# A stage-by-stage recurrence with a feed-forward net in its gaps: p's rows in three pieces, low parts moved ahead, output parts placed among the h32 stages

## What is computed

```python
# q, p: [8, 512]; drive: x[:, t, :], t = 0..255; dt = 0.01
def derivative(q, p, drive):
    dq = q - q ** 3 / 3.0 - p + drive + jnp.tanh(q) @ coupling.T + bias
    dp = 0.08 * (q + 0.7 - 0.8 * p)
    return dq, dp
# 256 steps of the classical four-stage Runge-Kutta method, q and p clipped to +-20 after each
# q_trace: [8, 256, 512], the q after every step
w_gu, w_down = dequant_fp4(gate_up), dequant_fp4(down)      # 2816 x 512, 512 x 1408
gate, up = split(q_trace @ w_gu.T)
y = (silu(gate) * up) @ w_down.T
out = x + y / sqrt(mean(y * y, axis=-1) + 1e-6)
```

## Time and profile before

| | |
|---|---|
| median of 3 runs | 1520.15 us (1519.74 to 1520.77) |
| the profiled execution | 1519.87 us, span 1518.0 us |
| busy: PE, PE's weight loads, DVE, ACT, GpSimd | 94%, 93%, 95%, 47%, 1% |
| instructions on DVE | 10781 |
| chain that ended last | PE 89% (L518 53%, L295 22%, L307 14%), DVE 5% |
| PE products of the recurrence (L518) | 32768, mean 175 ns |
| granted TensorE clock | 0.999 over the span |

### The profile page before, as it was taken

The page is one execution under the profiler, slowest core; times in us unless marked ns, Lnnn a source line. Parts: engine busy times, 40 slices in busy tenths (PEclk is TensorE's granted clock), DMA queues, the critical chain, the costliest instruction groups (busy, mean ns, idle before and its releaser), DMA issues.

```text
span 1518.0 us, 90291 instructions
## 1 busy us (share of the span) xinstructions
PE 1424.1 (94%) x36992; PEld 1408.7 (93%) x36992; DVE 1434.8 (95%) x10781; ACT 718.9 (47%) x4836; POOL 12.2 (1%) x38
## 2 busy tenths in 40 slices
PE   0277999999999999999999999999999999999998
PEld 0166999999999999999999999999999999999998
DVE  6999999999999999999999999999999999999991
ACT  2144445445454544545454454545445455544541
POOL 0000000000000000000000000000000000000000
PEclk9999999999999999999999999999999999999999
DMA  9500000000000000000000000000000000000000
GB/s 243 138 7 4 15 7 8 22 8 21 4 8 21 8 21 8 21 4 7 21 8 22 7 22 4 8 21 8 22 8 21 7 4 22 7 21 8 22 4 22
DMA packets 13520, 32.67 MB, mean 22 GB/s; under 512 B 1712, under 2 KB 6064, under 8 KB 12976
## 3 DMA queue, kind: packets, MB, share of 16 engines
q1 hardware_dynamic: 13104, 26.89, 6.7%
HBM read 22.69 MB, written 4.19 MB: 18 GB/s over the span
## 4 chain that ended last, share of the span: by engine, by line
PE 89%; DVE 5%; ACT 0%; issue 0%; POOLq 0%; DVEq 0%; POOL 0%; ACTq 0%
PE scan_ps L518 53%; PE gu_ps L295 22%; PE y_ps L307 14%; DVE th L590 1%; DVE q_stage L626 1%; DVE with_q L584 1%; DVE q_stage L628 1%; DVE q_sq L594 0%; DVE scan_ps L602 0%; DVE p_part L584 0%; DVE q_cub L597 0%; DVE with_p L584 0%; ACT th L556 0%; DVE q_raw L628 0%; DVE q_raw L626 0%
## 5 line engine op out<-in xcount | busy, mean ns | idle before, releaser
L518 PE MATMUL scan_ps<-th,wscan 128*128 128x32 f16 (+1 forms) x32768 | 1015.9, 175 | 87.6 <-ACT th L556 87.0
L518 PEld LDWEIGHTS scan_ps<-th,wscan 128*128 128x128 f16 x32768 | 937.9, 96 | 102.6 <-ACT th L556 95.1
L556 ACT ACTIVATE th<-q_stage 128x16 f16<-128x16 f32 x1536 | 318.5, 207 | 527.6 <-DVE q_stage L626 527.6
L295 PE MATMUL gu_ps<-hist,wffn 128*128 128x128 f32 x2816 | 503.3, 284 | 0.0
L295 PEld LDWEIGHTS gu_ps<-hist,wffn 128*128 128x128 f32 x2816 | 393.9, 192 | 0.0
L590 DVE TENSOR_TENSOR th<-t,th 128x16 f16<-128x16 f32 x2048 | 352.6, 172 | 1.1 <-ACT t L558 0.6
L307 PE MATMUL y_ps<-wffn,h 128*128 128x128 f32 x1408 | 323.6, 313 | 0.0
L558 ACT ACTIVATE t<-q_stage 128x16 f32<-128x16 f32 x1536 | 305.8, 199 | 0.0
L556 ACT ACTIVATE th<-q_raw 128x16 f16<-128x16 f32 x512 | 106.2, 207 | 220.8 <-DVE q_raw L626 182.6
L307 PEld LDWEIGHTS y_ps<-wffn,h 128*128 128x128 f32 x1408 | 209.5, 189 | 0.4 <-DVE h L323 0.4
L373 ACT ACTIVATE sum_r<-dr,constant 128x64 f32<-128x64 f32 x528 | 174.1, 332 | 7.8 <-DMA dr<-drive 7.8
(11 more groups left out here) (33 smaller groups left out, 539.3 us busy)
## 6 DMA issues: line engine op xcount, KB each, us to landing
raw<-packed SPq DMA_DIRECT2D x11, 768.0 KB, 9.0
dr<-drive SPq DMA_DIRECT2D x34, 128.0 KB, 2.5
sc<-scales SPq DMA_DIRECT2D x11, 384.0 KB, 9.3
xres<-x SPq DMA_DIRECT2D x16, 256.0 KB, 3.5
out<-osb SPq DMA_DIRECT2D x16, 256.0 KB, 2.9
coup<-coupling_t SPq DMA_DIRECT2D x1, 1024.0 KB, 15.0
q_raw<-cond_t SPq DMA_DIRECT2D x1, 16.0 KB, 1.6
bias<-bias_t SPq DMA_DIRECT2D x1, 2.0 KB, 1.7
```

What stands on the lines that cost most here:

```text
L295: i = nc.tensor.matmul(gu_ps[b][:, half * P:(half + 1) * P], wffn[:, u, j * P:(j + 1) * P], hist[1 - f.parity][:, kt].rearrange("p t b -> ...
L518: i = nc.tensor.matmul(to if both else to[:, 0], wscan[:, w, part, kt, cols], moving if both else moving[:, 0], start=first, stop=last, sk ...
L556: nc.scalar.activation(th[s % 2][:, c, 0, :], q[:, c, :], ACT.Tanh, scale=1.0 / S).then_inc(now.tanh_hi, 1)
```

## The change

`add_p` is cut in three: rows 1 and 2 (64 elements) at the head of a step's first stage, row 3 (32 elements) behind the last additions of the second stage, row 0 (32 elements) where all four stood, in the last stage of the step before. The third stage's first instruction now waits for row 3. In a step's last stage the order becomes `low_part` 0, p4, `low_part` 1, `cube`. `norm_out` may only take stages that are 1 modulo 4 and have no `h32` in either block: 81, 93, 109 and 121, that is 17, 29, 45 and 57 of the next block. With them, the wait for `other_cleared` moves from step 12 to step 15 (stage 60). DVE has 22 counted instructions for each step in place of 20.

```diff
-LOCALS = STEPS * 20
+LOCALS = STEPS * 22
...
-        first = self.norm_sum + 3
-        first += -first % 4
-        self.norm_out = {first + 4 * n: n for n in range(KT)}
+        taken = {s % STAGES for s in ready}
+        free = [s for s in range(self.norm_sum + 3, 2 * STAGES) if s % 4 == 1 and s % STAGES not in taken]
+        self.norm_out = {s: n for n, s in enumerate(free[:KT])}
...
-            def add_p(step):
-                p_rows = p_state[:, :, :].unsqueeze(1).to_broadcast([P, ROWS, KT, B])
-                return add(with_p[:, :], p_rows, P_ALL, sum_r[:, step % STEPS])
+            def add_p(step, first, rows):
+                p_rows = p_state[:, :, :].unsqueeze(1).to_broadcast([P, rows, KT, B])
+                return add(with_p[:, first:first + rows], p_rows, P_ALL, sum_r[:, step % STEPS, first:first + rows])
...
-                if t == STEPS - 4 and before:
+                if t == STEPS - 1 and before:
                     dve.wait_ge(now.other_cleared, 1)
                 if t == 0 and before:
                     dve.wait_ge(before.local, LOCALS)
-                ffn_part(s)
+                add_p(t, 1, 2)
...
                 add_q(with_q2[0], 2, BY_Q2, q2, with_q1[1][:, :, :])
+                row3 = add_p(t, 3, 1)
                 finish(s)
 
                 s = 4 * t + 2
+                dve.wait_ge(now.local, row3)
                 add_q(with_q1[2], 3, BY_Q1, q1, with_p[:, 3])
-                ffn_part(s)
...
                 squared = square(3, q4)
+                low_part(s, 0)
                 p4 = add(p_part[3][:, :, :], p_part[2][:, :, :], P_SUM[3], q4)
-                low_part(s, 0)
+                low_part(s, 1)
                 dve.wait_ge(now.local, squared)
                 cubed = cube(3, q4)
-                low_part(s, 1)
...
-                add_p(t + 1)
+                add_p(t + 1, 0, 1)
                 finish(s)
```

## The result

The changed kernel takes **1573.84 us** (median of 4 runs, 1569.38 to 1576.39) against 1520.28 us (1519.74 to 1520.77), a ratio of 1.035 with a 95% interval of 1.032 to 1.038: 53.6 us slower. The profiled execution took 1576.39 us with a span of 1574.6. Its runs are 7 us apart, those of the kernel before 1 us; what is known of that is told under parts_only.

The account below looks back on a forecast made before the run. A loop of reduce, tanh on ACT, low parts on DVE and PE's products sets each stage. 1519.9 - 10.1 (gains) + 47.7 (wait) + 15.4 (clock) = 1572.9, about 1573 us; 8 in 10 range 1553 to 1588.

Parts of the forecast that it names:

- the chain: Last output part, store, xres load, GpSimd's clear, then DVE's wait: 7.5 us (7.0 to 8.2), with three stages to run.
- case (c): Rival: xres lands up to 1 us a block later beside the drive's load, clock pays twice; 1593 us, chance 0.07.
- Case (b): Rival: GpSimd's clear is early, chain under 4.1 us, DVE does not stand at stage 60; 1510 us, chance 0.05.
- the wait: DVE stands 3.4 us at stage 60 in each of blocks 2 to 15, 47.7 us in all (40 to 57).
- case (d): Rival: pieces cost what they bring, the 10.1 us gain goes, wait as forecast; 1583 us, within the forecast's 0.60.
- Clock: PE's clock gate falls to half rate in the stage 60 waits, in up to 14 places; 15.4 us.
- case (a): Rival: the wait is there but the clock stays up; 1558 us (1550 to 1567), chance 0.27.
- The last stage: Each step's last stage: 0.03 us saved, 0.02 at steps 7 and 15, 0.06 in block 0; 7.9 us together.
- The pieces: Rows 1 and 2 free before the clip; row 3 fits the second stage's gap, 0.6 us in all behind h32.
- a later clip: At step 1, expected to roughly cancel the second wait removed at step 12.
- The output parts: Moved from first to second stages: a block pays 0.24 us in place of 0.42, 2.5 us saved (1 to 5).
- Gains: Wanted part of the change: 7.9 from last stages + 2.5 from output parts - 0.3 = 10.1 us.

Follow-up runs that it names:

- parts_only: Kernel before with only the output parts in stages 17, 29, 45 and 57 and the other_cleared wait at step 15; 1576.85 us, ratio 1.038.
- parts_early: Changed kernel with the four output parts in stages 17, 29, 33 and 45 instead of 17, 29, 45 and 57; 1508.37 us, ratio 0.992.
- no_low_parts: parts_early with p4, low part 0, cube, low part 1 back in their old order; 1515.90 us, ratio 0.9974.
- keep_busy: Changed kernel plus 12 unused f32 products on PE at stage 60 of blocks 2 to 15, inside the wait; 1556.90 us.
- load_first: Changed kernel with SP issuing the load of xres ahead of the store of osb, not behind its landing; 1509.80 us, ratio 0.993.
- early_parts_only: Kernel before with only its output parts in stages 17, 29, 33 and 45 and the wait at step 15; 1517.77 us, ratio 0.9986.

## Why the prediction was right, and where it was off

**Mechanism.** Each link of the chain stood as predicted. The blocked instruction starts 7.46 us after the output part in the block shown (7.55 predicted), and only in blocks 2 to 15. Over these it is 7.08 to 8.84, where 7.0 to 8.2 was said: GpSimd's wait reaches 8.23 us in one block, over the 7.60 read from the kernel before, while the median went down. So case (c), that the chain grows because the drive's load runs beside it, shows in the median not at all. Case (b), a clear that comes early, is refuted by the wait itself, and case (d), pieces that cost what they bring, by parts_early and no_low_parts. keep_busy and parts_early put the wait at 48.5 us against 47.7, load_first shows that its length is the two transfers in a row, and parts_early that nothing of it is lost when they have time.

**Clock.** Predicted at 1.1 us for each wait, 15.4 in all; keep_busy gives 16.9, or 1.2 each, and 17.9 with the fall that it still has. Of the 1.2 some 0.2 lie in stage 60 itself, whose last products come at the lower level (5069 against 4810 ns, of which 0.07 us are DVE's longer wait). The granted clock fell in all 14 waits. The term was the least sure one: case (a), that it stays up, had 0.27, on the argument that no fall is recorded in the loop before. There was no pause long enough to try it. What decided for the forecast, the fall 2.1 us after PE's last product, was the right row to go by. The Trainium skill, "TensorE: Matmul & The Clock Gate", Part 1, says that an idle PE goes back to half rate and has to earn the full one again in each turn of a loop that waits; the trace agrees, with 0.50 in the windows from 789 to 793 us.

**The last stage.** 0.03 us for a plain one: 1382 to 1351 or 1353 ns. At steps 7 and 15 0.02 was taken and 0.024 came. In block 0, 88.8 to 87.9 us for its 64 stages, 0.9 against 1.0.

**The pieces.** Rows 1 and 2 in front of the clip cost nothing (stage 8: 1368 and 1369). Row 3 fits the gap of the second stage; where an `h32` stands ahead the stages differ by -1 to +11 ns (stage 37: 1352 to 1363), but for stage 33, which is 20 ns shorter because two blocks before have it 0.14 and 0.16 us longer than the others. At step 1, with a second wait on the clip, a later clip was expected; stage 4 gained 10 ns instead.

**The output parts.** A part in stage 29, 45 or 57 costs 67 ns and not 80, and the one in stage 17 nothing. The four cost 0.20 us a block in place of 0.41 (16: 1574 to 1487; 20, 24, 28: 1476 to 1369), 2.9 us in all against 2.5. Why it is 13 ns less for each was not looked into.

**The sum.** Gains 10.1 predicted; parts_early, which has all of them and one dearer place, has 12 (1520.4 to 1508.4). The three terms predicted were 10.1, 47.7 and 15.4, those measured 12, 48.5 and 16.9. That the sums lie 1 us apart is partly luck: gain and clock were each 1.5 to 2 us too small, with opposite signs, and the four runs lie 7 us apart.

## What to carry to other kernels

When work is moved later in a program, follow what hangs on it through every queue to the instruction that finally waits: here a part of 0.34 us had two transfers, a clear and the busiest engine behind it, and its distance to the wait shrank from 20 stages to 3. Price such a wait twice where PE stands in it, once for its length and once for the clock behind it. Two instructions that are each free in a gap are not free together: measure the gap, and count all that is put into it.

## What the runs showed of the hardware that was not expected

First, the lower clock hardly slows the recurrence itself, but with the f32 products behind it a stage goes from 1.34 to about 1.9 us, so that the same fall of the clock costs much or little by what PE does next. Block 0, without such products, runs at 1.37 us a stage with its 32 records in 1.04 to 1.10 us; they take 1.06 us above where the clock column has 0.50, and 0.96 where it has 1.00, so I read block 0 as the lower level, though the column shows 1.00 there. Second, in keep_busy a pause of 1.53 us with products ahead of it passed without a fall, and one of 1.63 us did not: the clock fell there, by the windows at about 1240.4, 1.4 us after PE had gone on. In the changed kernel all 14 pauses, 2.7 to 4.5 us long, had a fall. Third, the change's runs spread over 7 us, and those of parts_only, with 14 falls too, over 3.3; kernels without falls spread over 1 to 3.1 (1 in parts_early, 2.6 in load_first; the kernel before 1 in 4 runs, 3.1 in 9 others), keep_busy, with one, over 1.5. So only the 7 us stand out. Fourth, single stages took 0.35 us more in a few places of a run: stage 48 of blocks 1 and 9 before, stage 31 of blocks 2 and 10 in early_parts_only and, the same, in parts_only. Their cause was not tested.
